# Two decoder blocks on one core: the last stage's first block placed inside the attention's last block, and one written plan for all four stages

## The reference

```python
x = L0_attn_x                                   # 1 x 4096 x 512
x = _layernorm(x + _L0_attn_ref(x, ...))        # linear attention, 16 heads, chunks of 64
x = _layernorm(x + _L0_ffn_ref(x, ...))         # gated, fp8 products, hidden 2048
x = _layernorm(x + _L1_attn_ref(x, ...))        # causal softmax attention in 1024s, one head of 128
x = _layernorm(x + _L1_ffn_ref(x, ...))         # base product + shared and routed low-rank parts
```

```python
base_out = einsum('bsd,df->bsf', x, W_base) + b_base
shared_out = einsum('bsr,rf->bsf', einsum('bsd,dr->bsr', x, A_s), B_s)
gates = softmax(einsum('bsd,de->bse', x, W_router) + b_router)     # 6 experts
topk_w, topk_i = top_k(gates, 2)
w_per_e = sum(topk_w[..., None] * one_hot(topk_i, 6), axis=2)
h = einsum('bsd,edr->bser', x, A_r)                                # rank 16 for each expert
return base_out + shared_out + einsum('bser,erf->bsf', h * w_per_e[..., None], B_r)
```

## Time and profile before

| | |
|---|---|
| median of 3 runs | 1561.22 us (1559.19 to 1561.75) |
| the profiled execution | 1564.32 us |
| its span in the profile | 1562.6 us |
| PE busy | 1475.6 us (94%) |
| DVE busy | 1005.5 us (64%) |
| ACT busy | 736.5 us (47%) |
| POOL busy | 341.0 us (22%) |

### The profile page before, as it was taken

One profiled execution on the slowest core, in us unless ns is written; L12 is line 12 of the kernel. 1 busy time (PEld: TensorE's weight loads), 2 busy tenths in 40 slices (PEclk: granted clock), 3 DMA queues, 4 the chain that ended last, 5 costly groups with the idle time before them and its releaser, 6 DMA issues.

```text
span 1562.6 us, 23839 instructions
## 1 busy us (share of the span) xinstructions
PE 1475.6 (94%) x9484; PEld 1012.5 (65%) x9484; DVE 1005.5 (64%) x1961; ACT 736.5 (47%) x1040; POOL 341.0 (22%) x256
## 2 busy tenths in 40 slices
PE   8999999999999977899999999977999999989998
PEld 6677777777777755344555555455666666557886
DVE  3355545464545545988778777843888888556665
ACT  4333333333333322977877886743434444442333
POOL 0021112121111222000000000000666776750001
PEclk9999999999999989999999999989999999999999
DMA  7203131303122140001100110022100000000112
GB/s 262 79 27 107 33 101 53 105 28 106 51 83 64 42 169 21 28 1 55 55 27 28 54 55 0 1 68 81 39 1 1 1 1 1 1 1 28 55 54 81
DMA packets 43904, 79.93 MB, mean 51 GB/s; under 512 B 7073, under 2 KB 14881, under 8 KB 42386
## 3 DMA queue, kind: packets, MB, share of 16 engines
q1 hardware_dynamic: 43794, 78.41, 14.8%
HBM read 53.24 MB, written 25.17 MB: 50 GB/s over the span
## 4 chain that ended last, share of the span: by engine, by line
PE 58%; issue 22%; DVE 14%; ACT 3%; POOL 2%; DMA 0%; SPq 0%; DVEq 0%; POOLq 0%; ACTq 0%
PE psum L142 12%; PE psum L144 11%; PE psum L143 11%; PE psum L1328 5%; DVE sm L465 3%; PE psum L612 2%; PE psum L1306 2%; PE psum L638 2%; PE psum L633 2%; PE psum L989 2%; PE psum L627 2%; PE psum L982 1%; DVE c_mx L1249 1%; PE psum L642 1%; PE psum L647 1%
## 5 line engine op out<-in xcount | busy, mean ns | idle before, releaser
L982 PE MATMUL psum<-early,high 128*128 128x512 fp8e4 x1024 | 234.5, 381 | 11.5 <-DVE low_r L954 4.2
L982 PEld LDWEIGHTS psum<-early,high 128*128 128x128 fp8e4 x1024 | 98.0, 98 | 133.9 <-ACT early L863 6.7
L1182 POOL TENSOR_TENSOR c_ls<-c_ls,c_pr 128x512 f32<-128x512 f32 (+2 forms) x136 | 162.3, 1193 | 57.4 <-ACT c_pr L1225 48.0
L411 POOL TENSOR_TENSOR rms<-ms,mhalf 128x16 f32<-128x16 f32 x32 | 93.2, 2911 | 365.6 <-DVE ms L474 365.6
L1225 ACT ACTIVATE c_pr<-c_sc 128x512 f32<-128x512 f32 (+2 forms) x144 | 85.3, 594 | 151.5 <-DVE c_sc L1264 139.4
L142 PE MATMUL psum<-Qh,Kh 128*128 128x512 f32 (+1 forms) x272 | 142.4, 523 | 0.0
L1328 PE MATMUL psum<-c_pr,V 128*128 128x512 f32 (+2 forms) x288 | 138.1, 565 | 3.1 <-ACT c_pr L1225 1.9
L1264 DVE TENSOR_TENSOR c_sc<-psum,c_mb 128x512 f32<-128x512 f32 (+2 forms) x144 | 92.2, 642 | 50.1 <-PE psum L144 37.5
L989 PE MATMUL psum<-high,b_act 128*128 128x512 fp8e4 x512 | 115.2, 379 | 0.0
L142 PE MATMUL psum<-early_r,high_r 128*128 128x512 f32 x256 | 106.7, 417 | 5.8 <-DVE early_r L437 5.8
L143 PE MATMUL psum<-Ql_r,Kh 128*128 128x512 f32 (+1 forms) x272 | 105.6, 388 | 0.0
(11 more groups left out here) (227 smaller groups left out, 3253.7 us busy)
## 6 DMA issues: line engine op xcount, KB each, us to landing
low<-x_dram SPq DMA_DIRECT2D x9, 1024.0 KB, 5.6
wst<-in_L_ffn_w_gating SPq DMA_DIRECT2D x16, 512.0 KB, 4.6
xs<-in_L_attn_x SPq DMA_DIRECT2D x8, 1024.0 KB, 8.0
xt<-in_x_turned SPq DMA_DIRECT2D x7, 1024.0 KB, 4.8
x_dram<-xs SPq DMA_DIRECT2D x7, 1024.0 KB, 4.7
x_dram<-low SPq DMA_DIRECT2D x5, 1024.0 KB, 4.3
wst<-in_L_ffn_w_linear SPq DMA_DIRECT2D x16, 256.0 KB, 4.8
high<-x_dram SPq DMA_DIRECT2D x4, 1024.0 KB, 6.8
```

The costliest lines, as they stand in the source:

```text
L411: nc.gpsimd.tensor_tensor(rms[:, :], ms[:, :], const["mhalf"][:, 0:H], ALU.pow).then_inc(*done)
L982: last = t.matmul(out[:, h, :], w8g[:, tile + k, (2 * m + h) * P:(2 * m + h + 1) * P], x8[:, u, k, :], start=k == 0, stop=k == DC - 1)
L1182: nc.gpsimd.tensor_tensor(ls[:, i % 2, q0:], ls[:, i % 2, q0:], pr[:, g % SLOTS, q0:], ALU.add).then_inc(*L.done(*name))
```

## The change

It does five things.

1. One list `plan` now holds the jobs of all four stages in the order in which they are meant, and each engine takes its pieces of it; the hand-written cuts at the end of the program are gone.
2. D's first block is placed within C's last block: `x(0, k)` behind pv 14 to 17, `h(0)` behind pv 19, `hN(0)` behind pv 21, the gates in six pieces behind pv 22 to 27, `hT(0)` behind pv 29.
3. C's last row sums and outputs stand between D's products, and D's order of blocks 0 and 1 is new.
4. The bias product of C is a job of its own.
5. All engines of a job are cut at the same place. So the pieces of D's weights on ACT stand behind exp (i, k + 2), where those of DVE stand behind sub (i, k + 2) as before; and B's first four DVE steps stand with PE's `u(0, 0)`.

The core of it:

```diff
+def pieces(plan, stages, engine):
+    at = {s: 0 for s in stages}
+    run, stop = None, 0
+    for s, job in plan:
+        if run is not None and (s != run or job[0] == "ahead"):
+            yield stages[run], stages[run][engine][at[run]:stop]
+            at[run], run = stop, None
+        if job[0] == "ahead":
+            if job[1] == engine:
+                yield stages[s], job[2]
+        else:
+            run, stop = s, stages[s]["cuts"][job][engine]
...
-    order = [("x", 0, k) for k in range(DC)] + [("h", 0)] + [("x", 1, k) for k in range(DC)]
-    order += [("hN", 0), ("rb", 0, 0), ("rb", 0, 1), ("rb", 0, 2), ("hT", 0), ("h", 1), ("rr", 0, 0), ("hN", 1),
-              ("rr", 0, 1), ("rr", 0, 2), ("rb", 0, 3), ("rr", 0, 3), ("hT", 1)]
+    order = [("x", 0, k) for k in range(DC)] + [("h", 0), ("hN", 0)] + [("gate", 0, n) for n in range(6)] + [("hT", 0)]
+    order += [("rb", 0, 0), ("rr", 0, 0)] + [("x", 1, k) for k in range(DC)] + [("rb", 0, 1), ("h", 1), ("rr", 0, 1), ("hN", 1)]
+    order += [("rb", 0, 2), ("rr", 0, 2), ("rb", 0, 3), ("rr", 0, 3), ("hT", 1)]
...
+    gate_pieces = [gate[:3], gate[3:6], gate[6:10], gate[10:14], gate[14:19], gate[19:]]
...
-            w = (3, 7, 6, 7)[name[2]]
+            w = (7, 4, 5, 0)[name[2]]
...
-        splits = [(3, 0)] + [(6, 3 * k) for k in range(DC + 1)]
+        plan = part("A", None, ("o", last, 3))
+        plan += part("B", None, ("x", 0, 1)) + part("A", ("o", last, 3), ("y", last, 2))
+        plan += part("B", ("x", 0, 1), ("u", 0, 0)) + part("A", ("y", last, 2), None)
+        plan += part("B", ("u", 0, 0), ("VT", last - 1)) + [("C", ("ahead", "dve", 0))] + part("B", ("VT", last - 1), None)
+        plan += [("D", ("ahead", "pool", 0))]
+        opening = {("pv", last, 14 + n): job for n, job in [(k, ("x", 0, k)) for k in range(DC)] + [(5, ("h", 0)), (7, ("hN", 0)), (15, ("hT", 0))]}
+        opening.update({("pv", last, 22 + n): ("gate", 0, n) for n in range(6)})
+        splits = {("s", 3, 2): 0, **{("s", 6, 3 * k + 2): k + 1 for k in range(DC + 1)}}
+        for job in part("C", None, ("y", last - 1, CH - 1)) + part("C", ("y", last - 1, CH - 1), ("pv", last, NB * CH - 1)):
+            plan.append(job)
+            if job[1] in splits:
+                plan += [("D", ("ahead", "act", splits[job[1]])), ("D", ("ahead", "dve", splits[job[1]]))]
+            if job[1] in opening:
+                plan.append(("D", opening[job[1]]))
+        plan += part("D", ("hT", 0), ("rb", 0, 0)) + [("C", ("L", last))] + part("D", ("rb", 0, 0), ("rr", 0, 0))
+        plan += part("C", ("L", last), ("y", last, 1)) + part("D", ("rr", 0, 0), ("rr", 0, 2)) + part("C", ("y", last, 1), None)
+        plan += part("D", ("rr", 0, 2), None)
```

More of the change, by code:

```diff
@@ L68, in at @@
         return self.sem, (block + (self.ahead - back)) * len(self.names) + self.index[name]
[L71 to L89, removed]
 def wait_for(eng, block, *needs):
@@ L102, in wait_for, with cuts_of, plan_banks @@
         eng.wait_ge(*steps.at(block, *name, back=back))
[L105 to L137, removed]
+def cuts_of(job_counts):
+    return {job: dict(zip(("pe", "act", "dve", "pool"), counts)) for job, counts in job_counts}
+def plan_banks(plan, stages):
+    last = {}
+    for s, job in plan:
+        stage = stages[s]
+        if job not in stage["banks"]:
+            continue
+        use = stage["uses"][job]
+        banks = stage["banks"][job]
+        stage["free"][job] = [last[w] for w in banks if w in last and last[w] != use]
+        for w in banks:
+            last[w] = use
+def pieces(plan, stages, engine):
+    at = {s: 0 for s in stages}
+    run, stop = None, 0
+    for s, job in plan:
+        if run is not None and (s != run or job[0] == "ahead"):
[6 more added lines that the diff above has]
+            run, stop = s, stages[s]["cuts"][job][engine]
+    if run is not None:
+        yield stages[run], stages[run][engine][at[run]:stop]
 def split3(tensor, out, hi_w, lo_w, hi_x, lo_x, first, last):
@@ L325, in stage_a, with bank_of @@
             if kind in quad_reader:
-                w = 0
+                banks[name] = range(DC)
                 steps, step = quad_reader[kind]
-                use = (steps, (step, *name[1:], 1))
-            elif (kind, b) == ("q", 0):
-                w, use = name[2], (A, ("qe", *name[1:]))
-            else:
[L332 to L343, removed]
+                uses[name] = (steps, (step, *name[1:], 1))
+                continue
+            steps, step = reader[kind]
+            uses[name] = (steps, (step, *name[1:]))
+            if (kind, b) == ("q", 0):
+                banks[name] = (name[2],)
+            elif kind == "st":
+                banks[name] = (7,)
+            else:
+                banks[name], turn = (4 + turn % 3,), turn + 1
+        def bank_of(*name):
+            return bank[banks[name][0]]
         def sync_engine(sp, load_next):
@@ L730, in stage_b @@
         pending, norms = None, []
-        for name in order:
+        for n, name in enumerate(order):
             kind, b = name[0], name[1]
@@ L777, in stage_b @@
                   "K": (V, "Kl"), "Q": (V, "Ql"), "VT": (A, "vt"), "V": (A, "V")}
[L778 to L782 removed]
+        banks, uses, free = {}, {}, {}
         n_front = n_back = 0
@@ L1052, in stage_c @@
     pro_dve = s.sem("c_pro_dve")
-    pro_pe = s.sem("c_pro_pe")
     scale = float(P) ** -0.5
@@ L1442, in stage_d, with bank_of @@
     L = Steps(s.sem("d_pool"), pool_order, 0)
-    M = Steps(s.sem("d_pe"), order, 0)
-    def bank_of(kind, b, c=0):
-        if kind == "x":
-            return (0, 1, 2, 5)[c]
-        return (3, 6, 7)[(CH * b + c) % 3] if kind in ("rb", "rr") else 4
+    M = Steps(s.sem("d_pe"), pe_order, 0)
+    reader = {"x": (V, "xl"), "h": (A, "hn"), "hN": (V, "hr"), "hT": (V, "hl")}
+    banks, uses, free = {}, {}, {}
+    for name in pe_order:
+        kind, b = name[0], name[1]
+        if kind == "x":
+            banks[name] = ((0, 1, 2, 5)[name[2]] if b else (3, 7, 5, 3)[name[2]],)
+            uses[name] = (V, ("xl", *name[1:]))
+        elif kind in ("rb", "rr"):
+            banks[name] = ((3, 6, 7)[(CH * b + name[2]) % 3],)
+            uses[name] = (V, ("y", *name[1:]))
+        else:
+            banks[name] = (4,)
+            steps, step = reader[kind]
+            uses[name] = (steps, (step, b, None) if step == "hr" else (step, b))
+    def bank_of(*name):
+        return bank[banks[name][0]]
     def moments(b, c):
```

272 lines of the change are left out of this document (126 added, 146 removed).

## The result

| | before | changed |
|---|---|---|
| median (range) | 1561.49 us (1559.19 to 1561.92) | 1571.10 us (1570.36 to 1571.75) |
| the profiled execution | 1564.32 us | 1571.75 us |
| its span | 1562.6 us | 1570.0 us |

The ratio is 1.0064, with a 95% interval of 1.0047 to 1.0082: slower, as forecast (1567.0), but by 9.6 us instead of 5.8, and just outside the range (1561.0 to 1571.0). The two spans differ by 7.4 us only, since the profiled execution of before was 2.8 us over its median and that of the changed kernel 0.7.

A forecast was written before the change was run, and what follows sets the result against it. PE was taken to set the pace in attention blocks 6 and 7. Passage -4.5, gates +1.2, A's end +1.7, weights +2.0 (block 3) and +5.4 (block 6) make +5.8; on 1561.2 that gives 1567.0 us, range 1561.0 to 1571.0.

The forecast's parts named there:

- Weights in block 6: Block 6, five pieces of D's weights: DVE waits for ACT's late exponential and rounding; loss 5.4 us, bounds 3 and 7.
- the second piece: Block 6, second piece of D's weights: DVE waited for POOL's `bo` anyway, so nothing added.
- the last two pieces: Block 6, fourth and fifth pieces of D's weights: exponentials late relative to PE, 1.3 and 0.8 us more.
- one wait of some 2.5 us for a "pv": Expected sign in PE's list of waits: one "pv" waiting for `c_pr` some 2.5 us.
- Weights in block 3: Block 3, D's weights: DVE stands still for ACT's late rounding, PE waits for its second "mx"; loss 2.0 us.
- slow clock: Block 3: PE's slow clock, named only for the upper bound, 3.5 us, of the 2.0 us loss.
- End of A: End of stage A: four DVE steps ahead of `ol` make it 2.25 us later; loss 1.7 us, bounds 0.5 and 3.2.
- B hides some: Start of stage B: it hides some of the 1.7 us loss from stage A's end; lower bound only, 0.5 us.
- Passage and gates: Passage from C to D: waits and slow clock fall from 10.5 to 6.0 us, gain 4.5; block 7's gates: loss 1.2.
- The new waits: Passage from C to D: PE waits 1.8 us at `h(1)`, 2.4 at `rr(1,0)`, 1.8 at `h(2)`.
- all steps would wait a sum: Rival, block 7: six gate steps each wait for a POOL sum, 5.2 instead of 1.2 us; 1572 us, chance 0.12.
- the places where the order of ACT or DVE changes: Places the prediction went through, after PE's waits, to see what stood still or was in reserve; no size.

The follow-up runs named there:

- e1: Changed kernel with ACT's six roundings of D's weights back ahead of the third exponential in blocks 3 and 6; 1561.6 us, ratio 1.0006 to the kernel before.
- e2: Kernel before with only ACT's six roundings of D's weights late, behind the exponential of tile k+2 and its norm; 1572.4 us, ratio 1.0064.
- e11: Changed kernel with ACT's roundings back where they were, except the second of block 6, which stays late; 1560.4 us, ratio 1.0007 to the kernel before.
- e7: Changed kernel with POOL's sums over block 7's last ten tiles made over 128 columns instead of up to 512; 1569.8 us, ratio 1.0062 to the kernel before.
- e9: Changed kernel with the product s(3,3) issued four times instead of once, filling PE's wait in block 3; 1570.6 us, ratio 1.0067 to the kernel before.
- e4: Changed kernel with B's first four DVE steps back behind all of A's; 1570.8 us, ratio 1.0065 to the kernel before.
- e10: Changed kernel with ACT's roundings, B's first DVE steps and C's bias product back where they were; 1557.5 us, ratio 0.9987 to the kernel before.

## Why the prediction was right in direction and short in size

*Weights in block 6* (+5.4, measured +6.0). Right in cause, place and size: e1 takes it all away, e2 brings it back alone, e11 shows the second piece free. The missing 0.6 us are the last two pieces (1.6 and 1.2 instead of 1.3 and 0.8), where DVE stood still for 1.9 and 2.0 us. One sign came out otherwise: instead of one wait of some 2.5 us for a "pv" there are three, of 0.8, 1.0 and 0.8 us, and waits for a "mx" of 1.1, 1.3 and 1.4.

*Weights in block 3* (+2.0, measured +3.9). The mechanism was right, and so was its size: where block 3 has the same slow stretch behind mb(3) as before, PE waits 1.6 us (e7) and 2.0 (e2), and in e7 the block is 1.7 longer than before. Two things of the clock came on top. Behind the wait PE ran at the lower clock, which is worth 1.9 to 2.2 us (39.5 instead of 37.3 in e7 and 37.6 in e9, which had no slow matmul there). And how long PE waits depends on the stretch behind mb(3): slow there, PE comes late and waits 1.6 to 2.0; fast, it waits 2.9 (changed). Against e1 and e11 (34.6), which are fast there too, the changed kernel loses 4.9. The prediction had the slow clock only in the bound of this term ("slow clock", 3.5).

*End of A* (+1.7, measured +0.7). The 2.25 us for `ol` are there (4.41 instead of 2.16), but the step "B hides some", which I had used for the lower bound alone, should have been in the sum: PE's 0.79 us wait for A's last chunk at B's start in the trace before is gone after.

*Passage and gates* (-4.5 + 1.2 = -3.3, measured -3.2). The sum is right in part by luck. The new waits are 1.5, 1.9 and 1.5 instead of 1.8, 2.4 and 1.8, and the gates cost 0.6 instead of 1.2: 1.5 us better. The slow clock behind `h(2)` took back 2.2; without it (e4) the piece gains 5.7. By these numbers the gain should be 2.6, so 0.6 us of the 3.2 are in no term. The mechanism of the gates was right (e7); that all steps would wait a sum was rightly rejected.

*The step that failed.* There are two. First, the prediction went through "the places where the order of ACT or DVE changes", took "transposes, products and steps" as the same in number, and did not compare PE's own order at C's start. The bias product, which the description calls only "a job of its own", moved there from ahead of the first "mx" to behind mb(0). No term stands for it; the piece measured +1.7 us, of which 0.4 to 0.7 are the place at the same clock and the rest a longer stretch at the lower clock. Second, in the sum each new wait of PE of 1.5 us or more was priced by its length. The kernel before showed the price of the clock behind one wait, and I used it for the wait that went away, and for the new ones in the bounds only. It would have added 1.9 in block 3, and 2.2 behind `h(2)`, where errors of 1.5 in the other direction hid it. Added up, the missing 3.4 us (5.8 to 9.2) are 1.7 at C's start, 1.9 in block 3, 0.6 in block 6 and 0.1 in the passage, less 1.0 at A's end.

*What stays open.* The sum of the pieces is made from single executions. In e1 it says 1.4 us faster than before and the medians say 0.3 slower; in e10 it says 6.0 faster and the medians 2.4. The kernel before is itself 3 us slower in its profile than in its median, and no trace of a faster execution of it exists here, so I can't say in which piece these 3 us lie. The same holds for the 0.4 us between the 9.2 of the pieces and the 9.6 of the medians. The 3 us go with time at the lower clock: executions of the kernel before with a span up to 1558 us have a mean granted clock of 0.985 to 0.987, those above 1562 us (the traced one too) 0.982 or 0.983. Why the clock falls behind some waits and not behind others of the same length was not found.

## What to carry to other kernels

When code that sets the order is rewritten, compare the order of each engine job by job, also for what the description calls a mere regrouping: here the side effect of one such regrouping (the roundings two tiles later, 9.9 us) cost more than the main idea gained. Cutting all engines of a job at the same place is wrong where one engine's step feeds another's: the feeder must stand ahead by as much as it was ahead before. And a forecast of a new wait on PE needs two prices, its length and, as an upper value, its length with a slow stretch behind it. The upper value is not always paid: in e2 some sixteen matmuls of the passage are slow instead of six, and the piece from mb(7) is 224.1 as before. Eight of them lie ahead of PE's wait for `hN(0)`, which shrank from 3.6 to 2.1 us.
